# Edge counting in a four-layer graph kernel: row one-hots made on GpSimd instead of VectorE

## The reference, cut to what matters

```
edge_index = [src, dst]                     # dst is sorted
x = layernorm(x + L0(x, edges))             # attention: softmax over the edges of a node
x = layernorm(x + L1(x, edges))             # mean of the neighbours
x = layernorm(x + L2(x, edges))             # convolution with edge weights of a small MLP
x = layernorm(x + L3(x, edges))             # attention with an edge MLP

L0:  s1 = Wh @ a1;  s2 = Wh @ a2
     e  = leaky_relu(s1[row] + s2[col]);  e = e - max(e)
     alpha = exp(e) / (segment_sum(exp(e), row)[row] + 1e-10)
     h' = elu(segment_sum(alpha * Wh[col], row))
L1:  mean of x[src] over the edges into a node, then two dense products
```

## Time and profile before

| what | us |
|---|---|
| median of 3 runs | 9076.38 (9073.87 to 9081.07) |
| the profiled execution | 9026.2 |
| its span | 9024.4 |
| TensorE busy | 7554.3 (84%) |
| VectorE busy | 6072.0 (67%) |
| ScalarE busy | 5237.7 (58%) |
| GpSimd busy | 3483.8 (39%) |

### The profile page before, as it was taken

The page is one execution under the profiler, slowest core; times in us unless marked ns, Lnnn a source line. Parts: engine busy times, 40 slices in busy tenths (PEclk is TensorE's granted clock), DMA queues, the critical chain, the costliest instruction groups (busy, mean ns, idle before and its releaser), DMA issues. The chain is left out here.

```text
span 9024.4 us, 195785 instructions
## 1 busy us (share of the span) xinstructions
PE 7554.3 (84%) x51013; PEld 5691.8 (63%) x51014; DVE 6072.0 (67%) x12579; ACT 5237.7 (58%) x9302; POOL 3483.8 (39%) x4082
## 2 busy tenths in 40 slices
PE   5999999888869998899989978777777877777774
PEld 3666666587769996666666655555656665566664
DVE  7888998899964446555555555556666666666666
ACT  3666666688857775444444433336666666566663
POOL 0000000000000001666666666664666666666665
PEclk8999999999989998899999887889999899889997
DMA  3333333466646662222222211113555555555554
GB/s 112 137 137 134 137 138 139 146 234 220 226 127 183 183 183 77 62 63 62 62 61 62 59 47 46 46 46 114 168 171 168 167 165 172 165 163 167 171 172 129
DMA packets 511185, 1177.42 MB, mean 130 GB/s; under 512 B 98171, under 2 KB 171308, under 8 KB 491685
## 3 DMA queue, kind: packets, MB, share of 16 engines
q1 hardware_dynamic: 381834, 858.67, 29.2%
q0 software_dynamic: 129280, 317.93, 12.6%
HBM read 899.64 MB, written 276.57 MB: 130 GB/s over the span
## 5 line engine op out<-in xcount | busy, mean ns | idle before, releaser
L2263 POOL DMA_INDIRECT att_kv_rows<-kv_dram,att_stage x1616 | 1657.1, 1025 | 1021.4 <-issue 679.0
L2002 POOL DMA_INDIRECT conv_rows<-y_dram,conv_stage x1616 | 1576.9, 976 | 876.3 <-issue 616.7
L1967 ACT ACTIVATE conv_hid<-conv_hid_ps 100x512 f32<-100x512 f32 x408 | 243.3, 596 | 1145.0 <-DMA y_dram<-mean_nodes_both 785.9
L695 PE MATMUL conv_part<-conv_msgs,conv_hot 128*128 128x256 f32 x3232 | 900.0, 428 | 5.0 <-issue 4.6
L842 PE MATMUL att_mlp<-mlp_feats,mlp_w 64*128 64x512 f32 x1568 | 534.6, 738 | 409.6 <-ACT mlp_hid L862 348.1
L851 PE MATMUL att_mlp<-mlp_w,mlp_hid 128*128 128x128 f32 x6272 | 770.9, 283 | 42.4 <-issue 24.4
L851 PEld LDWEIGHTS att_mlp<-mlp_w,mlp_hid 128*128 128x128 f32 x6272 | 748.4, 199 | 61.6 <-issue 39.6
L695 PEld LDWEIGHTS conv_part<-conv_msgs,conv_hot 128*128 128x128 f32 x3232 | 677.2, 221 | 105.5 <-issue 10.6
L235 PE MATMUL count_ps<-count_cols,count_rows 128*128 128x392 bf16 x3920 | 730.1, 332 | 8.5 <-DVE count_cols L201 8.5
L862 ACT ACTIVATE mlp_hid<-att_mlp,mlp_b 128x512 f32<-128x512 f32 x784 | 498.4, 684 | 379.7 <-PE att_mlp L842 256.2
L2035 PEld LDWEIGHTS conv_w_ps<-conv_w,conv_hid 100*128 100x128 f32 x3248 | 458.8, 217 | 396.4 <-issue 365.7
(11 more groups left out here) (278 smaller groups left out, 16280.7 us busy)
## 6 DMA issues: line engine op xcount, KB each, us to landing
c_dram<-count_counts SPq DMA_DIRECT2D x392, 392.0 KB, 2.4
mean_counts<-c_dram SPq DMA_DIRECT2D x343, 448.0 KB, 3.4
w_dram<-mlp_w SPq DMA_DIRECT2D x404, 256.0 KB
att_w_rows<-w_dram SPq DMA_DIRECT2D x404, 256.0 KB
soft_counts<-c_dram SPq DMA_DIRECT2D x98, 1024.0 KB, 4.8
mlp_feats<-in_feats SPq DMA_DIRECT2D x405, 192.0 KB
soft_counts<-c_dram SPq DMA_DIRECT2D x49, 1088.0 KB, 5.0
att_lanes<-lo_dram SPq DMA_DIRECT2D x404, 128.0 KB
```

The lines of the kernel that those rows point to most:

```text
L695: ins = nc.tensor.matmul(part, c.hot[:, s, t, :], rows[:, t, :], start=half == 0 and t == 0, stop=half == 1 and t == T - 1)
L2002: pool.indirect_dma_start(rows[:, s, t, :], None, y_dram, bass.IndirectOffsetOnAxis(ap=stage[:, s, t:t + 1], axis=0)).then_inc((gathered[s ...
L2263: pool.indirect_dma_start(kv_rows[:, s, t, :], None, kv_dram, bass.IndirectOffsetOnAxis(ap=stage[:, s, t:t + 1], axis=0)).then_inc((gather ...
```

## The change

The row one-hots go to GpSimd. VectorE keeps the column one-hots, the further tiles and the moving of its own lane numbers. GpSimd gets its own copy of the lane numbers (`row_lanes`, made by an iota at the start of the stage and moved on by GpSimd itself after every eighth block) and copies the five keys of each block into `keys`. It makes five one-hots of 128x128 in five instructions. TensorE waits for one more semaphore, `rows_done`.

```diff
+        self.row_lanes = sb("row_lanes", [P, VB, P])
+        self.keys = sb("keys", [P, 2, T0])
...
 def count_hots(nc, dve, c, at, i, v):
...
-    nc.vector.tensor_tensor(c.rows[:, b], at.lanes[:, v].unsqueeze(1).to_broadcast([P, T0, P]),
-                            over(at.row_key[:, bass.ds(first, T0)], [P, T0, P], 2), ALU.is_equal)
     for t in range(T0):
         ins = nc.vector.tensor_scalar(c.cols[:, b, t], at.cols[:], at.col_key[:, bass.ds(first + t, 1)], None, ALU.is_equal)
     ins.then_inc(c.hot_done, 1)
...
+def count_rows(nc, pool, c, at, i, v):
+
+    k, b = VB * i + v, v % 2
+    word = pool.value_load(at.words[:, bass.ds(k, 1)], min_val=0, max_val=2 ** 31 - 1)
+    first = nc.s_assert_within(pool.snap(word & 2047), 0, NT - T0, ...)
+
+    pool.wait_ge(c.counted, k + 1)
+    nc.gpsimd.tensor_copy(c.keys[:, b], at.row_key[:, bass.ds(first, T0)]).then_inc(c.keys_copied, 1)
+    if v == 0:
+        pool.wait_ge(c.row_lanes_moved, i + 1)
+    pool.wait_ge(c.keys_copied, k + 1)
+    pool.sem_inc(c.row_turn, 1)
+    for t in range(T0):
+        ins = nc.gpsimd.tensor_scalar(c.rows[:, b, t], c.row_lanes[:, v], c.keys[:, b, t:t + 1], None, ALU.is_equal)
+    ins.then_inc(c.rows_done, 1)
+    if v == VB - 1:
+        pool.wait_ge(c.rows_done, k + 1)
+        pool.sem_inc(c.row_turn, 1)
+        nc.gpsimd.tensor_scalar(c.row_lanes[:], c.row_lanes[:], float(VB * P), None, ALU.add).then_inc(c.row_lanes_moved, 1)
...
     pe.wait_ge(c.gap_done, k + 1)
     pe.wait_ge(c.hot_done, k + 1)
+    pe.wait_ge(c.rows_done, k + 1)
...
+            @block.gpsimd
+            def _(pool):
+                nc.gpsimd.iota(c.row_lanes[:], pattern=[[P, VB], [1, P]], base=0, channel_multiplier=0,
+                               allow_small_or_imprecise_dtypes=True).then_inc(c.row_lanes_moved, 1)
+                with pool.Fori(0, NK // VB) as i:
+                    for v in range(VB):
+                        count_rows(nc, pool, c, at, i, v)
```

More of the change, by code:

```diff
@@ L175, in __init__ @@
         self.hot_done = sem("count_hot_done")
+        self.rows_done = sem("count_rows_done")
+        self.keys_copied = sem("count_keys_copied")
+        self.row_turn = sem("count_row_turn")
+        self.row_lanes_moved = sem("count_row_lanes_moved")
         self.hot_done_x = sem("count_hot_done_x")
@@ L210, in count_hots @@
             nc.vector.tensor_scalar(c.cols_x[:], at.cols[:], at.col_key[:, bass.ds(t, 1)], None, ALU.is_equal).then_inc(c.hot_done_x, 1)
+def count_rows(nc, pool, c, at, i, v):
+    k, b = VB * i + v, v % 2
+    word = pool.value_load(at.words[:, bass.ds(k, 1)], min_val=0, max_val=2 ** 31 - 1)
+    first = nc.s_assert_within(pool.snap(word & 2047), 0, NT - T0, skip_runtime_bounds_check_because="windows begin at tiles")
+    pool.wait_ge(c.counted, k + 1)
[11 more added lines that the diff above has]
+        nc.gpsimd.tensor_scalar(c.row_lanes[:], c.row_lanes[:], float(VB * P), None, ALU.add).then_inc(c.row_lanes_moved, 1)
 def count_measure(nc, dve, c, at, i, v):
```

## The result

The changed kernel takes 9373.1 us (median of 4 runs, 9369.02 to 9377.56) against 9075.39: ratio 1.0327, 95% interval 1.0309 to 1.0345. It is slower by 3.3%, about 298 us, where no change was forecast (9074, range 9058 to 9280). One execution of a later run (the one with deeper buffers) took 24,273 us at a granted clock of 0.30; its median is taken without it.

What follows compares the result with a forecast made beforehand. TensorE was taken to bound the counting stage. A gain of 2.8 us from shorter waits for VectorE, with nothing added by TensorE's extra waits or GpSimd, gave 9076.4 - 2.8 = 9073.6, called 9074 us, range 9058 to 9280.

Steps and rivals of the forecast that it cites:

- What bounds the kernel before: Counting stage: VectorE follows TensorE, which is 95% busy against 89%; relieving VectorE gains 2.8 us.
- the 63.4 us behind ScalarE: Counting stage: TensorE's 46 waits for ScalarE's MLP activation, 63.4 us together, forecast to stay.
- so I take the cheap end: GpSimd's row one-hot priced from iota and cast: 0.11 us of work, 0.19 from start to start.
- dear end: GpSimd's row one-hot priced from a tensor_tensor: 0.30 us of work, 0.38 from start to start.
- first test: Does GpSimd keep up: 17.8 of 33.19 us per iteration, 31.8 with a 0.35 us wait before each one-hot; it fits.
- Each us of GpSimd's work can cost VectorE one: Contention in the counting stage: up to 6.1 us per iteration, against 6.6 taken away and 10.1 idle.
- Rows 9 and 10: Profile rows: a GpSimd cast waits out two VectorE instructions; a VectorE instruction takes 2.97 us beside GpSimd's tensor_tensors.
- second test: What GpSimd costs VectorE: VectorE busy or held 29.2 of 33.19 us per iteration, as much as now.
- starved: Rival: GpSimd gets no turn between VectorE's queued instructions and misses block windows; 64 us, about 9138, 15%.
- dear: Rival: GpSimd's comparison costs 0.30 us of work per one-hot; priced at 150 us, 9150 to 9280, 20%; over 9280, 10%.
- 0.94 us per block for the keys: GpSimd, each block: what waits for its copy of the keys starts 0.94 us after the copy's end.
- The signs of being wrong: Changed profile: one-hot over 0.35 us undisturbed, TensorE waiting for `count_rows` or `count_cols` in many iterations, iteration over 33.5 us.

Runs made afterwards that it cites:

- the one with deeper buffers: Changed kernel with four buffers instead of two for row one-hots and keys: 9325.5 us, ratio 1.0288.
- first run: Kernel before with the row one-hots left out and nothing added on GpSimd: 9050.57 us, ratio 0.9989.
- run with the copy: Kernel before with the copy of block 7's counts out of PSUM moved from ScalarE to VectorE: 9093.79 us, ratio 1.0031.
- run with a constant: Changed kernel with GpSimd's one-hots compared with a constant in place of the key from SBUF: 9226.4 us, ratio 1.0168.
- the run with VectorE out of the way: Changed kernel with one of five column one-hots per block on VectorE and the fused maximum left out: 9078.81 us, ratio 1.0013.
- second run: Changed kernel, but VectorE makes the row one-hots TensorE uses; GpSimd makes unread ones for 38 of 49 iterations: 9192.68 us, ratio 1.0141.

## Why the prediction was wrong

- **What bounds the kernel before: right.** TensorE sets the pace of the stage, VectorE's relief is worth a few us by itself, and it leaves the 63.4 us behind ScalarE untouched (first run: 63.5). One thing the prediction did not see is that VectorE at 89% has nothing to give either: 1.9 us more of work and waiting on its queue in each iteration make the kernel 30 us slower (run with the copy).
- **The step that failed: "so I take the cheap end"**, 0.11 us of work and 0.19 from start to start for one row one-hot. Undisturbed it is 0.594 (2.94 for five, so 0.59 each), three times the value taken and over 1.5 times the prediction's dear end. The iota and the cast were the wrong neighbours. The move of the lane numbers, 1024 elements, takes 2.77 at best (taken: 1.02). If both follow one line, it is (2.774 - 0.594)/896 = 2.4 ns per element, near the tensor_tensor's 2.3, and about 0.28 us besides, of which 0.07 is the key (run with a constant). That is an estimate from two points of different operations. By it the dear end had the rate about right and missed most of the fixed part.
- **The price alone would not have done it.** "GpSimd may wait 0.35 us before each" was the right form of the first test with wrong numbers. With the true price the undisturbed work is 8 x 3.29 + 2.8 = 29.1 us and still fits; the run with VectorE out of the way shows it. What does not fit are the waits: 953.5/30.1 = 31.7 us of one-hots per iteration against 40 x 0.594 = 23.8, so 7.9 us of waiting, and the copies, the move and what GpSimd idles bring it to 39.8.
- **"Each us of GpSimd's work can cost VectorE one": the wrong side.** In the changed kernel VectorE's column one-hots grow by 54 ns, GpSimd's row one-hots by 215. Rows 9 and 10 showed both sides; the second test counted VectorE's, up to 6.1 us per iteration, of which 40 x 0.054 = 2.2 came. The rival named "starved" had the mechanism, GpSimd waiting out VectorE, at the cheap price; the one named "dear" had nearly the price, and it even worked out the product, an iteration of 40.7 us and 370 us over, where 39.7 and 307 were measured. The prediction then took that down to 150 us and gave 10% to anything over 9280. The nearness of 40.7 is luck in part: its 0.94 us per block for the keys was too dear and its 0.73 per waited one-hot too cheap (0.809).
- **Smaller terms.** 0.94 us for the wait on the copied keys: 0.20 in most rows. The late start (7.6 us) and the late end (3.8) were put at nothing, though the kernel before has a pair of MODIFY_POOL_CONFIG ahead of GpSimd's line 940, with 9.0 us from there to the first instruction (at 2576.4):

```profile
L940 POOLq MODIFY_POOL_CONFIG  x2: 11/11/11, 2567.4 to 2567.4; - x2
```

- **The signs of being wrong.** All three came: a one-hot over 0.35 us, many waits for `count_rows`, an iteration over 33.5. But that last limit told nothing, since the kernel before is itself at 33.5 in the mean.
- **The clock.** The prediction said that it might fall if TensorE waited often, and it did, to 0.94. TensorE's counting matmuls are busy 796.6 us instead of 730.1. It is a consequence and hardly a cause: with four buffers GpSimd next to never waits for TensorE and the loss is smaller by 35 us only, so the pace that TensorE's clock can set for GpSimd is worth no more than that.

The Trainium skill (SBUF — State Buffer, section "SBUF: two separate sides") says that a VectorE instruction in a two-port mode or with two inputs in SBUF and a GpSimd instruction exclude each other. The runs that leave out VectorE's work agree: without four of the five column one-hots and without the maximum, GpSimd's median falls from 721 to 603 ns. Its other statement, that whoever starts first holds the pair, does not by itself give the asymmetry of 54 against 215 ns; that is this case's measurement, and why it comes out so is open.

## What to carry to other kernels

Price a moved instruction by the same operation on the new engine, or else take the dearest neighbour and say so; here a cast and an iota were no guide to a comparison. And price it together with its waits: neither the price nor the waits alone made the loss. Before moving work between VectorE and GpSimd, count the instructions of VectorE that will meet it: here moving two fifths of the row one-hots brought VectorE nothing at all. And an engine at 89% beside a bound of 95% is no reserve: first take away the wait that TensorE really has, here by a change of order on ScalarE that gave 35 us. An iteration is measured as a mean over many, not as one.

## What the runs showed of the hardware

- GpSimd's tensor_scalar (is_equal, f32 in, bf16 out, 128x128) takes 594 ns, 521 with a constant; its cast of 896 elements takes 929. So the number of elements alone does not make the price: 128 elements of the one cost two thirds of 896 of the other.
- Where both engines are nearly always at work (second run, both 95% busy), the GpSimd instruction goes from 594 to 999 ns and VectorE's column one-hot from 417 to 477. VectorE has the better of it.
- A pair of MODIFY_POOL_CONFIG on GpSimd's queue is followed by 5.6 to 9.0 us in which GpSimd does nothing: 6.6 to 7.5 us ahead of the iota that opens the stage and 5.6 to 5.8 ahead of the partition_all_reduce, in all eight kernels with tensor_scalars on GpSimd, and 9.0 ahead of line 940 in the kernel before. Moving work to GpSimd brought two such pairs, one on the way in and one on the way out. The Trainium skill (GPSIMD Engine Reference, section "2.1 Instruction dispatch") states about 6 us, without a visible instruction, for the first call after code is loaded; the 5.6 to 5.8 us agree with it, the others are somewhat longer.
